# Attention with a sign layer on one core: query projections stand behind the weighing of even duos instead of between the scores of odd duos

## The chip, the core and the metric

The kernel runs on one core of one Trainium2 chip. The metric is the device time in microseconds (us) of one execution. The engines are TensorE (PE, with its weight loads as PEld), VectorE (DVE), ScalarE (ACT), GpSimd (POOL) and SyncE (SP, which issues all DMAs here).

## What is computed

Sixteen batches of 1024 rows of 256 numbers go through a layer norm, then through an attention of 16 heads of 16 columns, whose keys and values are the same for every batch, and through a dense layer whose weights are only signs. The reference, cut to what matters:

```python
xn = layernorm(x)                                  # x: (16, 1024, 256)
q = relu(xn @ Wq.T + bq); k = relu(keys @ Wk.T + bk); v = relu(values @ Wv.T + bv)
a = softmax(q_h k_h^T / 4) v_h                     # 16 heads h of 16 columns, 1024 keys
y = clip((xn @ sign(Wf).T) * scale + bias, -100, 100)
out = x + (a, laid out head by column by row, + xn) + y
```

## The kernel before, in words

**Half steps.** A batch is worked on in two half steps (`hh` 0 and 1), eight heads in each. What runs side by side in a half step belongs to different heads: the scores, exponentials and weighing of the heads `att`; the maxima of the heads after them, which the softmax of the next half step needs; the end of the heads `last`; and six or four small jobs on the next rows. Each engine has its own in-order program with a `half_step`, run for all batches from a loop (`run`, L364). With the lead-in there are 15 half steps with `hh` 0 that have scores and jobs, and 15 with `hh` 1.

**Duos.** A half step is 32 duos. The order of TensorE's work in a duo is written out in `half_step` (L766): first scores (`scores`, L588, two matmuls of 51 rows that run at once on the two halves of the array), maxima "between", second scores, maxima "before", the weighing (`weigh`, L602, eight instructions), and maxima "behind". Eight maxima, here n0 to n7 (`OCTET`, L267), are spread over an even and an odd duo by `STANDS` (L269) and `maxima_of` (L282): an even duo has n0 ahead of its weighing and n1, n2 behind it; an odd duo has n3 between the scores, n4, n5 ahead of the weighing and n6, n7 behind it. Each is one matmul of 48 rows and 512 columns (L633) into one of three banks of PSUM, the ring (L156). DVE reduces seven of the eight (L959; the one called "join" is L934, on n6), ACT takes the eighth, n2, which is a difference (L822). A matmul waits until the bank that it takes over was read, so n4 waits for the reduction of n1, and n5 for ACT on n2.

**Score tiles.** The scores go into two tiles of two banks each, used in turn, and ACT's exponentials read them (L806). A job also takes the next tile in turn (`plan`, L334; `tile`, L583), so a job behind the weighing of an even duo stands in the tile of that duo's first scores, and the odd duo's second scores wait until ACT has read the job's result.

**Jobs.** `JOBS` (L246) lists them and `JOB_DUOS` (L248) gives each its duo. With `hh` 0: four dense jobs (L677 and L679, eight matmuls of 256 columns each) and two projections of queries (L662, L664, L666, six matmuls of 512 columns each). With `hh` 1: two turns (transposes, L654) and two projections. In `plan` a turn or a projection stands between the two pairs of scores, a dense job behind the weighing. ACT copies a job's result out: L841 for a turn, L850 for a projection, L856 for a dense job. ACT's order in a duo is: first exponential, a job "between", second exponential, a job "behind", the difference n2 if the duo has it, and in the duos 9, 17, 25 and 1 a copy of the weighed sums (L813). The weighing of an even duo needs all exponentials up to the odd duo before it.

**Who else is touched.** GpSimd splits the turned rows (`split_turned`, L1145, into xnT_high and xnT_low), which the projections with `hh` 1 read, and splits the projected queries (`split_queries`, L1156) after `finish` (L1212). SyncE loads the split queries for the next heads (`load_queries`, L442), but not before the scores of duo 16 (`scored`, L543 and L547). DVE takes the reciprocals of the sums (L991) at the end of duo 7 of every half step.

The order that all this hangs on:

```python
for what in ("first", "between", "second", "behind"):
    if {"between": job and job[0] != "dense", "behind": job and job[0] == "dense"}.get(what, True):
        at[what] = tile % 2
        tile += 1
```

Of the kernel before, what the change touches and what calls it, by code (L numbers as in the profile page):

```python
# [27 lines left out]
def attention_block(nc: bass.Bass, x, keys_t, values_t, wq_t, bq, wk_t, bk, wv_t, bv, wf_t, scale, bias, out):  # L28
# [35 lines left out]
    with ctx:  # L64
        def sb(name, shape, dt):
            return ctx.enter_context(nc.sbuf_tensor(name, shape, dt))
# [34 lines left out]
        dense = sb("dense", [P, 2, BANK], FP32)  # L101
# [137 lines left out]
        def ring_order(jobs, first):  # L239
# [5 lines left out]

        JOBS = [[("dense", k, None) for k in range(2 * NA)] + [("project", a, 1) for a in range(NA)],  # L246
                [("turn", a, None) for a in range(NA)] + [("project", a, 0) for a in range(NA)]]
        JOB_DUOS = [[2, 4, 6, 8, 11, 13], [1, 3, 7, 9]]  # L248
        LEAD = 32
        ROWS_DUO = 26  # L250
        RECIP_UNIT = 14
# [30 lines left out]
        def maxima_of(d):  # L282

            n = LEAD + d // 2 * 8 + d % 2 * sum(STANDS[0])
            ends = [n + k for k in itertools.accumulate(STANDS[d % 2], initial=0)]
            return [range(*ends[k:k + 2]) for k in range(3)]
# [43 lines left out]
        def duo_job(hh, some, d):  # L330

            return JOBS[hh][JOB_DUOS[hh].index(d)] if some and d in JOB_DUOS[hh] else None

        def plan(hh, some, rows_duo):  # L334

            duos, tile, bank = [], hh * (UNITS + len(JOBS[0])), 0
            for d in range(DUOS):
                at = {}
                job = duo_job(hh, some, d)
                for what in ("first", "between", "second", "behind"):  # L340
                    if {"between": job and job[0] != "dense", "behind": job and job[0] == "dense"}.get(what, True):
                        at[what] = tile % 2
                        tile += 1
                for n in itertools.chain(*maxima_of(d)):
                    at[n] = bank % RING
                    bank += 1
                if d == rows_duo:
                    at["rows"] = bank % RING
                    bank += 1
                duos.append(at)  # L350
            assert bank % RING == 0
            return duos
# [208 lines left out]
        def _(pe):  # L561
# [204 lines left out]
            def half_step(b, hh, now, att, last, prep, ahead):  # L766
                if hh == 0:
                    next_batch()
                some = ahead or (now and hh == 0)
                for d, at in enumerate(plan(hh, some, ROWS_DUO)):  # L770
                    job = duo_job(hh, some, d)
                    between, before, behind = maxima_of(d)
                    if att:
                        scores(b, hh, att, 2 * d, at["first"])
                    if now:
                        for n in between:
                            maxima(b, hh, n, at)
                    if "between" in at:
                        do_job(b, hh, *job, at["between"])
                    if att:  # L780
                        scores(b, hh, att, 2 * d + 1, at["second"])
                    if now:
                        for n in before:
                            maxima(b, hh, n, at)
                    if last if d < 2 else att:
                        weigh(*(last if d < 2 else att), (d // 2 - 1) % QUADS, d % 2)
                    if "behind" in at:
                        do_job(b, hh, *job, at["behind"])
                    if now:
                        for n in behind:  # L790
                            maxima(b, hh, n, at)
                        if d == ROWS_DUO:
                            turn_maxima(b, hh, at["rows"])
# [5 lines left out]
        def _(act):  # L799
# [104 lines left out]
            def half_step(b, hh, now, att, last, prep, ahead):  # L904
                some = ahead or (now and hh == 0)
                for d, at in enumerate(plan(hh, some, ROWS_DUO)):
                    job = duo_job(hh, some, d)
                    if att:
                        exponentials(*att, 2 * d, at["first"])
                    if "between" in at:  # L910
                        take_job(b, hh, *job, at["between"])
                    if att:
                        exponentials(*att, 2 * d + 1, at["second"])
                    if "behind" in at:
                        take_job(b, hh, *job, at["behind"])
                    for n in itertools.chain(*maxima_of(d)):
                        if now and is_difference(n):
                            take_difference(b, hh, n, at)
                    if last and d == 1:
                        take(*last, 3)  # L920
                    if att and d % 8 == 1 and d > 1:
                        take(*att, d // 8 - 1)
                    if now and d == ROWS_DUO:
                        take_rows(b, hh, ahead, at["rows"])
# [5 lines left out]
        def _(dve):  # L930
# [142 lines left out]
            def half_step(b, hh, now, att, last, prep, ahead):  # L1073
                for d, at in enumerate(plan(hh, False, ROWS_DUO)):
                    if prep and d == AGGREGATE_DUO:
                        dve.wait_ge(s_stats, (b + 2) * 8)
                    if now:
                        for n in itertools.chain(*maxima_of(d)):
                            if prep and d in STATS_DUOS and n % 8 in STATS_AHEAD:
                                statistics(b, *ROW_TILES[2 * STATS_DUOS.index(d) + STATS_AHEAD.index(n % 8)])  # L1080
                            reduce_bank(b, hh, n, at)
                            if n >= TILES and not is_difference(n) and reductions(n - TILES) <= 5:
                                split_maxima(b, hh, reductions(n - TILES) - 1,
                                             b * 2 * REDS + made(hh, TILES - 1))
                    if last and d == RECIP_UNIT // 2:
                        reciprocals(*last)
                    if prep and AGGREGATE_DUO <= d < AGGREGATE_DUO + 4:
                        for a, j in ROW_TILES[2 * (d - AGGREGATE_DUO):2 * (d - AGGREGATE_DUO) + 2]:
                            aggregate(a, j)
# [211 lines left out]
```

## Time and profile before

| | us |
|---|---|
| median of 3 runs | 2849.71 |
| the runs | 2847.73 to 2850.22 |
| the profiled execution, its own time | 2850.59 |
| its span in the profile | 2848.8 |
| mean granted TensorE clock | 0.983 of full speed |
| busy: PE, ACT, DVE, POOL | 2770.7, 2450.2, 2337.4, 938.4 |

Busy time of PE is the union of matmuls that overlap in time and whose ends are modelled, so it tells little of how much of it could be saved. What an engine really waited for is seen better in the start times of its instructions: in the views of this document the first column is the start in us from the beginning of the span, the second the duration, and square brackets hold the idle time of that engine ahead of the instruction, and what ended it. The chain of waits is the chain of work that ended last, followed back from the end of the execution.

### The profile page before, as it was taken

The page shows a single profiled execution, that of the slowest core. Times are in us where ns is not written, and L with a number is a line of the kernel's source. Part 1 is how long each engine was busy: PE and PEld are TensorE (multiplying, and loading weights), DVE is VectorE, ACT ScalarE, POOL GpSimd, SP SyncE. Part 2 cuts the span into 40 slices and gives each one's busy share as a digit, 9 for nine tenths or more (in the row PEclk, how much of TensorE's full clock was granted, in tenths as well). Part 3 has the DMA queues.
Part 4 walks back from the last instruction along what each step waited for, and adds up shares of the span by engine and source line. Part 5 has one row for each costly group of instructions (what it writes and reads, how often), then busy time and mean ns, then how long its engine had stood idle before and what let it go on. Part 6 is the DMA issues. An engine that isn't in the chain of part 4 may idle for free.

```text
span 2848.8 us, 61155 instructions
## 1 busy us (share of the span) xinstructions
PE 2770.7 (97%) x17860; PEld 1149.8 (40%) x17860; DVE 2337.4 (82%) x4578; ACT 2450.2 (86%) x2949; POOL 938.4 (33%) x845
## 2 busy tenths in 40 slices
PE   8899999999999999999999999999999999999996
PEld 4434444443444434444443444434444443444331
DVE  6788888888888888888888888888888888888940
ACT  4688888888888888888888888888888888888996
POOL 4304334242343314333242343314333242343001
PEclk8699999999999999999999999999999999999998
DMA  7111121121221121121121221121121121211111
GB/s 142 60 40 55 65 70 36 56 70 55 65 70 52 40 70 55 65 66 33 62 69 55 65 66 49 47 70 55 65 64 35 62 68 56 65 62 37 48 55 38
DMA packets 78637, 167.74 MB, mean 59 GB/s; under 512 B 28548, under 2 KB 32647, under 8 KB 76327
## 3 DMA queue, kind: packets, MB, share of 16 engines
q1 hardware_dynamic: 78374, 164.19, 19.2%
q8 instruction: 172, 2.82, 0.4%
q14 instruction: 91, 0.74, 0.1%
HBM read 36.71 MB, written 17.83 MB: 19 GB/s over the span
## 4 chain that ended last, share of the span: by engine, by line
PE 79%; issue 10%; DVE 7%; ACT 2%; POOL 1%; DVEq 0%; DMA 0%; POOLq 0%; ACTq 0%
PE value_ps L611 30%; PE ring L633 28%; PE score_ps L597 13%; DVE mx L959 5%; ACT probs L806 2%; PE score_ps L677 1%; PE score_ps L662 1%; PE score_ps L679 1%; PE score_ps L666 1%; PE score_ps L664 1%; PE ring L720 1%; POOL fin L1097 1%; PE score_ps L715 0%; DVE excess L934 0%; PE ring L700 0%
## 5 line engine op out<-in xcount | busy, mean ns | idle before, releaser
L806 ACT ACTIVATE probs<-score_ps 128x1024 f32<-128x1024 f32 x2048 | 1992.3, 1024 | 236.1 <-PE score_ps L597 229.9
L959 DVE TENSOR_REDUCE mx<-ring 128x1 f32<-128x512 f32 x2952 | 1900.1, 684 | 248.8 <-PE ring L633 224.5
L633 PE MATMUL ring<-kstack,qstack 48*128 48x512 f32 x3444 | 1168.4, 467 | 16.7 <-DVE mx L959 3.1
L611 PE MATMUL value_ps<-probs,vones 128*32 128x512 f32 x8192 | 1092.3, 605 | 1.1 <-ACT taken L813 0.4
L633 PEld LDWEIGHTS ring<-kstack,qstack 48*128 48x128 f32 x3444 | 490.1, 184 | 1071.0 <-DVE mx L959 1034.3
L597 PE MATMUL score_ps<-qstack,kstack 51*128 51x512 f32 x4096 | 814.1, 416 | 13.8 <-ACT probs L806 4.5
L934 DVE CUSTOM_DVE_ANT_0 excess<-ring,excess 128x512 f32<-128x512 f32 x512 | 353.1, 690 | 136.7 <-PE ring L633 119.1
L1097 POOL TENSOR_TENSOR dense<-dense,affine 128x512 f32<-128x512 f32 x128 | 164.4, 1284 | 866.7 <-ACT dense L856 865.2
L597 PEld LDWEIGHTS score_ps<-qstack,kstack 51*128 51x128 f32 x4096 | 393.6, 186 | 132.1 <-ACT probs L806 70.5
L822 ACT ACTIVATE excess<-ring 128x512 f32<-128x512 f32 x492 | 294.0, 597 | 1.4 <-PE ring L633 1.2
L611 PEld LDWEIGHTS value_ps<-probs,vones 128*32 128x32 f32 x8192 | 161.5, 108 | 320.7 <-issue 289.1
L633 PE MATMUL ring<-kdiff,qstack 48*128 48x512 f32 x492 | 244.7, 497 | 0.0
L1097 POOL TENSOR_TENSOR fin<-fin 128x1024 f32<-128x1024 f32 x32 | 76.3, 2385 | 406.2 <-DMA fin<-recip 406.1
L1097 POOL TENSOR_TENSOR varp<-meanvar,const 128x8 f32<-128x8 f32 x16 | 3.2, 203 | 467.5 <-DVE meanvar L987 467.5
L1097 POOL TENSOR_TENSOR fin<-base_cur,fin 128x1024 f32<-128x1024 f32 x32 | 93.3, 2915 | 3.7 <-POOL fin L1097 2.3
L633 PEld LDWEIGHTS ring<-kdiff,qstack 48*128 48x128 f32 x492 | 90.2, 183 | 0.1
L1097 POOL TENSOR_TENSOR xnT_high<-proj,const 128x1024 fp32r<-128x1024 f32 x30 | 56.9, 1898 | 100.8 <-ACT proj L841 100.8
L991 DVE RECIPROCAL sums<-sums 128x64 f32<-128x64 f32 x32 | 17.4, 543 | 86.3 <-DMA sums<-fin 86.3
L1097 POOL TENSOR_TENSOR xin<-xin,xn 128x1024 f32<-128x1024 f32 x32 | 76.3, 2385 | 28.2 <-DVE affine L1057 28.2
L1097 POOL TENSOR_TENSOR base_new<-xin,dense 128x512 f32<-128x512 f32 x64 | 82.2, 1284 | 2.6
L813 ACT ACTIVATE taken<-value_ps 128x512 f32<-128x512 f32 x128 | 77.0, 602 | 4.9 <-PE value_ps L611 2.1
L1097 POOL TENSOR_TENSOR parts<-proj,parts 128x512 fp32r<-128x512 f32 x62 | 79.5, 1283 | 4.9
(93 smaller groups left out, 1417.2 us busy)
## 6 DMA issues: line engine op xcount, KB each, us to landing
qstack<-parts SPq DMA_DIRECT2D x768, 64.0 KB, 2.5
fin<-taken SPq DMA_DIRECT2D x256, 128.0 KB, 2.9
xin<-x SPq DMA_DIRECT2D x16, 1024.0 KB, 5.1
base_cur<-base_new SPq DMA_DIRECT2D x16, 1024.0 KB, 5.3
fin<-recip SPq DMA_DIRECT2D x32, 512.0 KB
out<-fin SPq DMA_DIRECT2D x32, 512.0 KB, 2.6
qstack<-proj SPq DMA_DIRECT2D x256, 12.0 KB
kstack<-base_cur SPq DMA_DIRECT2D x16, 128.0 KB, 6.0
```

Of the source, the lines that this page charges most:

```text
L597: mm = pe.matmul(ps[:, side * BANK:(side + 1) * BANK], kstack[rows, ah * PAIRS + pair, tc * P:(tc + 1) * P], qstack[ah][rows, pair, a * BA ...
L611: mm = pe.matmul(value_ps[h4 * 32:(h4 + 1) * 32, :], vones[:, 2 * tp + c, hh * HALF + side * PAIRS + 2 * g + j, :, :], probs[:, q % 2 * GR ...
L633: pe.matmul(ps[:, :], qstack[nh][rows, pair, st * P:(st + 1) * P], keys, start=True, stop=True).then_inc(s_mm, 1)
L662: pe.matmul(ps[:, 0:BANK], wq_high[:, ic, cols], xnT_high[:, k, ic, :], start=(ic == 0), stop=False)
L664: pe.matmul(ps[:, 0:BANK], wq_high[:, ic, cols], xnT_low[:, k, ic, :], start=False, stop=False)
L666: mm = pe.matmul(ps[:, 0:BANK], wq_low[:, ic, cols], xnT_high[:, k, ic, :], start=False, stop=(ic == IC - 1))
L806: nc.scalar.activation(probs[:, q % 2 * GROUP + u % GROUP, :], score_ps[src][:, :], ACT.Exp, scale=EXP_SCALE).then_inc(s_probs, 1)
L813: nc.scalar.activation(taken[:, a % 2, :], value_ps[:, :], ACT.Copy).then_inc(s_taken, 1)
L822: nc.scalar.activation(excess[:, :], ring[at[n]][:, :], ACT.Relu).then_inc(s_relu, 1)
L934: nc.vector.tensor_tensor_reduce(out=over, in0=second, in1=over, op0=ALU.add, op1=ALU.max, scale=1.0, scalar=LOWEST, accum_out=most).then_ ...
L959: nc.vector.tensor_reduce(most, src[:, :], AX.X, ALU.max).then_inc(s_mx, 1)
L1097: return nc.gpsimd.tensor_tensor(dst, in0, in1, op)
```

## The change

The two projections of `hh` 0 move from the duos 11 and 13 to the duos 10 and 12, those of `hh` 1 from 7 and 9 to 6 and 8. In all four cases the place in the duo changes too: from between the two pairs of scores to behind the weighing, ahead of the maxima n1 and n2. The turns and the dense jobs stay. All engines that read `plan` follow: TensorE and ACT. No instruction is added or taken away.

```diff
-        JOB_DUOS = [[2, 4, 6, 8, 11, 13], [1, 3, 7, 9]]
+        JOB_DUOS = [[2, 4, 6, 8, 10, 12], [1, 3, 6, 8]]
...
                 for what in ("first", "between", "second", "behind"):
-                    if {"between": job and job[0] != "dense", "behind": job and job[0] == "dense"}.get(what, True):
+                    if {"between": job and job[0] == "turn", "behind": job and job[0] != "turn"}.get(what, True):
                         at[what] = tile % 2
                         tile += 1
```

## Rows read from the trace of the kernel before

**Rows 1.** Head of the page: busy us and share, and the granted clock.

```profile
PE 2770.7 (97%) x17860; PEld 1149.8 (40%) x17860; DVE 2337.4 (82%) x4578; ACT 2450.2 (86%) x2949; POOL 938.4 (33%) x845
...
PEclk8699999999999999999999999999999999999998
```

**Rows 2.** Chain of waits (start, us, what), hh 0: weighings of duos 8, 10, 12, 14.

```profile
1079.82 1.00 PE value_ps L611 x8
...
1085.87 1.00 PE value_ps L611 x8
...
1092.19 1.00 PE value_ps L611 x8
...
1098.49 1.00 PE value_ps L611 x8
```

**Rows 3.** Chain of waits, hh 1: weighings of duos 4, 6, 10 and 12.

```profile
983.84 1.00 PE value_ps L611 x8
...
988.75 1.00 PE value_ps L611 x8
...
1001.77 1.00 PE value_ps L611 x8
...
1006.70 1.00 PE value_ps L611 x8
```

**Rows 4.** Timeline, duos 8 and 9 of hh 0: a dense job behind the weighing.

```profile
1079.75 1.07 PE L611 MATMUL value_ps<-probs,vones 128*32 128x512 f32 x8
...
1080.75 0.39 PE L677 MATMUL score_ps<-wf_sb,xnT_high 128*128 128x256 f32 x1
...
1081.68 0.28 PE L679 MATMUL score_ps<-wf_sb,xnT_low 128*128 128x256 f32 x1
1081.89 0.18 PEld L633 LDWEIGHTS ring<-kstack,qstack 48*128 48x128 f32 x1
...
1082.00 0.60 ACT L856 ACTIVATE dense<-score_ps 128x512 f32<-128x512 f32 x1 [0.67 <-PE score_ps L679]
...
1082.42 2.56 DVE L959 TENSOR_REDUCE mx<-ring 128x1 f32<-128x512 f32 x4 [0.82 <-PE ring L633]
...
1082.49 0.59 ACT L822 ACTIVATE excess<-ring 128x512 f32<-128x512 f32 x1
1082.65 0.19 PEld L597 LDWEIGHTS score_ps<-qstack,kstack 51*128 51x128 f32 x2 [0.23 <-ACT dense L856]
...
1082.97 1.95 ACT L806 ACTIVATE probs<-score_ps 128x1024 f32<-128x1024 f32 x2
1083.17 0.26 PEld L633 LDWEIGHTS ring<-kstack,qstack 48*128 48x128 f32 x2 [0.34 <-DVE mx L959]
```

**Rows 5.** Timeline, duo 11 of hh 0: a projection between the scores.

```profile
1087.38 0.43 PE L633 MATMUL ring<-kstack,qstack 48*128 48x512 f32 x1
...
1087.74 0.50 PE L662 MATMUL score_ps<-xnT_high,wq_high 128*128 128x512 f32 x1
...
1089.00 0.40 PE L666 MATMUL score_ps<-xnT_high,wq_low 128*128 128x512 f32 x1
1089.32 0.19 PEld L597 LDWEIGHTS score_ps<-qstack,kstack 51*128 51x128 f32 x2 [0.36 <-issue]
...
1089.49 0.69 ACT L850 ACTIVATE proj<-score_ps,bq_sb 128x512 f32<-128x512 f32 x1 [0.61 <-PE score_ps L666]
```

**Rows 6.** Timeline, duos 8 and 9 of hh 1: the reciprocals, then the wait ahead of n3.

```profile
995.00 0.16 PEld L611 LDWEIGHTS value_ps<-probs,vones 128*32 128x32 f32 x8 [0.37 <-issue]
...
995.76 0.54 DVE L991 RECIPROCAL sums<-sums 128x64 f32<-128x64 f32 x1
...
996.91 0.18 PEld L633 LDWEIGHTS ring<-kstack,qstack 48*128 48x128 f32 x1 [0.61 <-DVE mx L959]
```

**Rows 7.** Timeline of GpSimd, hh 1: the second split of turned rows.

```profile
984.69 2.38 POOL L1097 TENSOR_TENSOR xnT_low<-proj,xnT_high 128x1024 fp32r<-128x1024 f32 x1
```

**Rows 8.** Timeline of GpSimd, hh 0: the end of `finish`, ahead of the split of queries.

```profile
1091.97 2.94 POOL L1097 TENSOR_TENSOR fin<-base_cur,fin 128x1024 f32<-128x1024 f32 x1 [0.17 <-POOL fin L1097]
```

## The prediction

> **What bounds the kernel now.** I read the head of the page first: PE is busy for 97% of the span, at full clock nearly throughout [rows 1]. ACT and DVE are busy for over 80% as well, so a busy share decides nothing. Then the chain of waits, by the starts of the weighings of even duos. The distance of two of them is the length of a pair of duos, and it repeats in all 15 half steps of a kind. A plain pair takes 4.92 us: 988.75 - 983.84 = 4.91, and 1006.70 - 1001.77 = 4.93 [rows 3]. A pair with a dense job takes 1085.87 - 1079.82 = 6.05 us, the two with a projection take 6.32 and 6.30 us [rows 2]. With hh 1 the two pairs with a projection take 1001.77 - 988.75 = 13.02 us together [rows 3]; the second begins at 995.07 (995.00 in the timeline, where this weighing stands 0.07 earlier), so they take 6.32 and 6.70 us [rows 3, 6]. So a job lengthens its pair by 1.1 to 1.8 us whatever else runs, and the question is how a projection's pair looks in the new place.
>
> Third, the timeline of a dense job behind the weighing, which is the place that the projections get [rows 4]. The reader is to see that TensorE goes from weighing to job 1.00 us after the weighing's start (1079.75 to 1080.75), from job to n1 at 1081.89, and that then a fixed train runs: DVE, which the job left idle for 0.82 us, starts on n1 at 1082.42; n4 needs n1's bank and starts at 1083.17, 1.28 us after n1, having waited 0.34 us for DVE. This wait is the price of the place: the work behind the job catches up with a reduction that starts late.
>
> **The change, part by part.** Nothing is added or removed: six matmuls on TensorE and one copy on ACT move, in four duos of a batch.
>
> *TensorE.* A projection takes 1087.74 to 1089.32 = 1.58 us from its first matmul to the next work [rows 5]; the dense job takes 1080.75 to 1081.89 = 1.14 us [rows 4]. From n1 to the next pair everything in the dense pair hangs on n1 and has the same instructions. So a pair with a projection behind takes 6.05 + 1.58 - 1.14 = 6.49 us, if ACT adds nothing.
>
> *ACT.* After a projection's last matmul starts, the copy starts 0.49 us later and takes 0.69 us, and the next work of TensorE starts after 0.32 us, so the copy ends 0.49 + 0.69 - 0.32 = 0.86 us after n1 starts [rows 5]. The dense copy ends at 1082.60, 0.71 us after n1 [rows 4]. So the odd duo's second scores, held 0.23 us by the dense copy, are held 0.15 us longer. They stand ahead of n4, which had 0.34 us to wait for DVE, and this covers it. The difference n2 is queued behind the copy on ACT and comes 0.15 us later too: with the dense job it ends at 1083.08, now at n1 + 1.34 us, and n5 needs its bank, just behind n4 at n1 + 1.28. That can cost 0 to 0.06 us; I take 0.03, so 6.52 us for the pair. If that cover were gone, the full 0.15 would be paid: 6.64 us and, with a little loss at the next exponentials, 6.67 at most. The exponentials behind the difference end at about 0.6 us later than the dense pair's 1084.92, still ahead of the even weighing that needs them (1085.80 in that timeline, also 0.47 later now) [rows 2, 4].
>
> *The reciprocals.* With hh 1 DVE's 0.54 us of reciprocals fall just ahead of n1 of duo 8, DVE is late, n3 waits 0.61 us, and the projection and second scores behind n3 are late with it: this is the 6.70 against 6.32 [rows 6]. Behind the weighing the projection stands ahead of n1, TensorE is busy with it while DVE catches up, as in the dense pair of duo 8 with hh 0, whose 6.05 us contain the same reciprocals. So this 0.38 us goes away, whatever else happens.
>
> *GpSimd and SP.* The projections of hh 1 read xnT_low, written at 987.07 [rows 7]; the new place begins at about 988.68 + 1.00 = 989.7, so no wait. The split of queries comes after `finish`, which ends at 1094.9 [rows 8], past the first projection in either place, and the loads wait for the scores of duo 16. The projection issues no DMA. Moving it half a duo earlier changes nothing on either queue: cost 0, covered by some 2.5 us and by the rest of the half step.
>
> *The sum.* hh 0: 2 x 6.52 - (6.32 + 6.30) = +0.42 us. hh 1: 2 x 6.52 - 13.02 = +0.02 us. Together +0.44 a batch, 15 times: +6.6 us. The profiled execution took 2850.59 us, so 2857.2; it stands 0.9 above the median of 2849.71, on which the forecast is given: 2856.3 us. A measurement can tell about 0.2%, 5.7 us, from no change; the sum passes this where a pair takes more than 6.505 us. My floor of 6.49 gives +4.8, 6.55 gives +8.4. So the likeliest case straddles this bound.
>
> The bounds of a pair: below, the 0.34 us wait of n4 vanishes altogether, 6.49 - 0.34 = 6.15 us; above, 6.67 us.
>
> **The rivals.**
>
> *No change worth measuring.* TensorE's wait for n1's reduction shrinks by some 0.04 to 0.1 us, since in the rows it is partly the way in which waits are seen rather than work, or the copy of a projection hides. A pair takes 6.41 to 6.50: 15 x (4 x 6.41 - 25.64) = 0 to +5.4 us, 2849.7 to 2855.1. For it: the floor lies only 0.08 above break-even. Against it: from n1 to the next weighing the dense pair takes 6.05 - 2.14 = 3.91 us [rows 2, 4], and the plain one, if its n1 follows the weighing after the same 1.00 us, 4.92 - 1.00 = 3.92.
>
> *Faster: fewer changes of the array's shape.* In the old place TensorE goes from n3, a matmul on half of the rows, to the whole array and back. The step from n3 to the projection takes 0.36 us (1087.38 to 1087.74), where one within the projection takes 0.25 (five from 1087.74 to 1089.00) [rows 5]. In the new place the projection follows the weighing, which uses all rows, and TensorE enters the dense job 1.00 us after the weighing's start, as it enters maxima. So 0.11 us of TensorE's time is saved per projection. If it reached the end of each pair, and the reciprocals' 0.38 as well, a batch would gain 4 x 0.11 + 0.38 = 0.82 us: -12.3 us, 2837.4. It decides where a pair gets below 6.41 - 0.09 = 6.32 us (a gain over 5.7 us). Against it: n4 waits for DVE in the new place, so what TensorE saves ahead of it is only saved if the reduction of n1 comes earlier, and that stands behind the whole job. In the old place n1's reduction had run during the projection.
>
> The Trainium skill, page "TensorEngine Tiling (Array Packing)", Key Properties, says that changing the tiling mode, not just the tile, drains TensorE. The old place has one such change more than the new, so the rule speaks for this rival; the longer step from n3 agrees with it, but the rows cannot show that the gain reaches the pair's end.
>
> *Slower, through ACT.* The copy, the difference and two exponentials in a row push n5 and the second scores late by the full 0.15 us: 6.67 us a pair, 15 x (26.68 - 25.64) = +15.6 us, 2865.3. For it: ACT has the longest work here. Against it: the dense pair has the same queue and shows 0.34 us of room.
>
> **How the numbers follow.** Dense-like pair 6.49 to 6.55 us: 0.55, of which 0.10 lies below the 0.2% bound. No change: 0.27. Faster: 0.10. Slower through ACT: 0.08. So faster 0.10, same 0.37, slower 0.45 + 0.08 = 0.53. The range leaves out the faster case and the upper half of the ACT case: from 2848.5, a shade below no change, to 2862.5. The likeliest case alone is 2854.5 to 2858.1.
>
> **What would show it.** After the change, the weighings of duos 6, 8 and 10 with hh 1 are 6.52 us apart, and those of 10, 12, 14 with hh 0 too; the wait ahead of n4 is 0.3 to 0.4 us on DVE in these pairs; the 0.61 us wait ahead of n3 is gone; the projection's copy ends 0.86 us after n1's start; plain and dense pairs keep 4.92 and 6.05. If the pair is 6.3 or less, the train behind n1 was not fixed, and I am wrong on the sign. If plain pairs change too, something outside of my sum has moved.

## The result, and the profile after

The changed kernel takes 2855.01 us (median of 20 runs, 2852.42 to 2858.05), the kernel before 2848.93 us over 20 runs: a ratio of 1.0022, 95% interval 1.0016 to 1.0028, or 6.1 us more. The forecast was 2856.3 us from a median of 2849.7, +6.6 us, slower. The span of the profiled execution is 2853.3 us against 2848.8.

The head of the page after the change shows why it isn't the view to read: nearly the same busy times [rows 1].

```profile
PE 2781.1 (97%) x17860; PEld 1161.0 (41%) x17860; DVE 2336.9 (82%) x4578; ACT 2441.8 (86%) x2949; POOL 938.4 (33%) x845
```

The chain of waits of the changed kernel (start, us, what), weighings of the duos 6, 8, 10 of hh 1, then of the duos 8, 10, 12, 14 of hh 0:

```profile
990.92 0.99 PE value_ps L611 x8
...
997.43 0.99 PE value_ps L611 x8
...
1003.92 0.99 PE value_ps L611 x8
...
1081.82 1.00 PE value_ps L611 x8
...
1087.87 1.00 PE value_ps L611 x8
...
1094.40 1.00 PE value_ps L611 x8
...
1100.93 0.99 PE value_ps L611 x8
```

With hh 0 the two pairs with a projection take 6.53 and 6.53 us, where they took 6.32 and 6.30 [rows 2]; the dense pair keeps 6.05. With hh 1 they take 6.51 and 6.49 us, 13.00 together, where it was 13.02 [rows 3]. So hh 0 loses 0.44 us a batch, hh 1 nothing, and 15 x 0.44 is 6.6 us.

The timeline of the changed kernel, duos 10 and 11 of hh 0 (start, us, engine, line, operation; in brackets the idle time ahead and what ended it):

```profile
1087.80 1.07 PE L611 MATMUL value_ps<-probs,vones 128*32 128x512 f32 x8
...
1088.80 0.50 PE L662 MATMUL score_ps<-xnT_high,wq_high 128*128 128x512 f32 x1
...
1090.38 0.18 PEld L633 LDWEIGHTS ring<-kstack,qstack 48*128 48x128 f32 x1 [0.36 <-issue]
...
1090.55 0.69 ACT L850 ACTIVATE proj<-score_ps,bq_sb 128x512 f32<-128x512 f32 x1 [1.16 <-PE score_ps L666]
...
1090.91 2.56 DVE L959 TENSOR_REDUCE mx<-ring 128x1 f32<-128x512 f32 x4 [1.66 <-PE ring L633]
...
1091.29 0.19 PEld L597 LDWEIGHTS score_ps<-qstack,kstack 51*128 51x128 f32 x2 [0.38 <-ACT proj L850]
...
1091.66 0.30 PEld L633 LDWEIGHTS ring<-kstack,qstack 48*128 48x128 f32 x2 [0.18 <-DVE mx L959]
...
1092.20 0.16 PEld L611 LDWEIGHTS value_ps<-probs,vones 128*32 128x32 f32 x8 [0.25 <-issue]
...
998.14 0.54 DVE L991 RECIPROCAL sums<-sums 128x64 f32<-128x64 f32 x1
...
1000.28 0.19 PEld L633 LDWEIGHTS ring<-kstack,qstack 48*128 48x128 f32 x1
```

The job takes 1.58 us (1088.80 to 1090.38). DVE is idle for 1.66 us and starts on n1 0.53 us after n1's matmul; n4 starts 1.28 us after n1 as in the dense pair [rows 4]; the copy ends at 1091.24, n1 + 0.86; the second scores start at n1 + 0.91. The last two rows are the duos 8 and 9 of hh 1: the reciprocals run while the projection does, and n3 stands at 1000.28 with no wait ahead of it, where it had 0.61 us [rows 6]. With hh 1 the copy comes a little sooner: it starts at 1000.05, 0.11 us after n1 at 999.94, and ends 0.80 us after it, where with hh 0 it starts 0.17 us after n1. So the pairs with hh 1 stay at 6.49 to 6.51 us.

### The profile page after: what moved, and what is told of

Its sections match the earlier page's. It is cut to its first block, busy times and chain, and to the rows that moved or that the text cites. A ratio compares the mean times of both kernels' runs of the same rounds, so it can differ in the third digit from the quotient of the medians.

```text
span 2853.3 us, 61155 instructions
## 1 busy us (share of the span) xinstructions
PE 2781.1 (97%) x17860; PEld 1161.0 (41%) x17860; DVE 2336.9 (82%) x4578; ACT 2441.8 (86%) x2949; POOL 938.4 (33%) x845
## 4 chain that ended last, share of the span: by engine, by line
PE 81%; issue 10%; DVE 5%; ACT 2%; POOL 1%; DVEq 0%; DMA 0%; POOLq 0%; ACTq 0%
PE value_ps L611 30%; PE ring L633 29%; PE score_ps L597 14%; DVE mx L959 4%; ACT probs L806 2%; PE score_ps L677 1%; PE score_ps L662 1%; PE score_ps L679 1%; PE score_ps L664 1%; PE score_ps L666 1%; PE ring L720 1%; POOL fin L1097 1%; PE score_ps L715 0%; DVE excess L934 0%; PE ring L700 0%
## 5 line engine op out<-in xcount | busy, mean ns | idle before, releaser
L850 ACT ACTIVATE proj<-score_ps,bq_sb 128x512 f32<-128x512 f32 x64 | 44.0, 688 | 70.7 <-PE score_ps L666 69.4
```

What stands on the lines that cost most here:

```text
L850: nc.scalar.activation(proj[:, k, :], score_ps[src][:, 0:BANK], ACT.Relu, bias=bq_sb[:, oc:oc + 1]).then_inc(s_qr, 1)
```

## The experiments

In kernels with `BEHIND` in the code the line numbers are two higher: L613 is the weighing, L961 the reduction, L599 the scores, L635 the maxima, L852 the projection's copy, L808 the exponentials, L815 the copy of the weighed sums and L993 the reciprocals. The edit of `plan` that is shown first stands in all of them, but for dense_between and best_mixed.

**One half step at a time.**

```diff
-        JOB_DUOS = [[2, 4, 6, 8, 11, 13], [1, 3, 7, 9]]
+        JOB_DUOS = [[2, 4, 6, 8, 10, 12], [1, 3, 7, 9]]      # h0_behind
+        BEHIND = [(0, 10), (0, 12)]
+        JOB_DUOS = [[2, 4, 6, 8, 11, 13], [1, 3, 6, 8]]      # h1_behind
+        BEHIND = [(1, 6), (1, 8)]
...
+                    late = job and (job[0] == "dense" or (hh, d) in BEHIND)
+                    if {"between": job and not late, "behind": late}.get(what, True):
```

> Only the two projections of hh 0 are moved, to duos 10 and 12 behind the weighing; those of hh 1 stay between the scores of duos 7 and 9. If the price is the late reduction of n1 behind the job, the two pairs of hh 0 take 6.52 us each instead of 6.32 and 6.30, those of hh 1 keep 6.32 and 6.70: 15 x 0.42 = +6.3 us against the kernel before. If the loss comes from hh 1 or from the starts of the half steps, this kernel is at +0 to +2 us.

> Only the two projections of hh 1 are moved, to duos 6 and 8 behind the weighing. By the same reason the pairs take 6.51 and 6.49 us instead of 6.32 and 6.70, since the reciprocals hide under the projection: 15 x (-0.02) = -0.3 us, and some 0.1 us more a batch if the last pair of the half step stays shorter, as the trace of the changed kernel shows: -0.3 to -2 us. The rival, that each move costs the same 0.2 us whatever stands there, gives +6 us.

Only hh 0: 2854.71 us against 2849.26, ratio 1.0020 (1.0011 to 1.0029), the whole loss. Only hh 1: 2849.41 us, ratio 1.0000 (0.9991 to 1.0010). In the chain of waits of h1_behind the weighings of the duos 6, 8, 10 of hh 1 start at 988.45, 994.96 and 1001.45: 6.51 and 6.49 us, as in the changed kernel. The parts add up, +5.45 and +0.15 us against +6.1 for both, within the intervals.

**The other two places.** Between the scores of even duos (`JOB_DUOS` of the change, `plan` of before), and behind the weighing of the old odd duos:

```diff
-        JOB_DUOS = [[2, 4, 6, 8, 11, 13], [1, 3, 7, 9]]
+        JOB_DUOS = [[2, 4, 6, 8, 10, 12], [1, 3, 6, 8]]      # even_between
+        BEHIND = []
+        BEHIND = [(0, 11), (0, 13), (1, 7), (1, 9)]          # odd_behind, old JOB_DUOS
```

> All four projections in the even duos 10, 12 and 6, 8, but between the two pairs of scores. If the place behind the weighing is what costs (DVE has nothing to do during the job), here DVE has n6 and n7 to reduce during the job, and the reciprocals too: the pairs take 6.2 to 6.35 us, all four alike, and the kernel is at 15 x (4 x 6.3 - 25.64) = -6.6 us (-2 to -12). If the even duo itself costs, the pairs take 6.5 us and the kernel stands at +5 us. If changes of the array's shape counted, this place would have one more than behind the weighing and be slower than it.

> The projections in their old odd duos, but behind the weighing, ahead of n6 and n7. DVE still has n4 and n5 to reduce during the job. No maximum ahead of the next weighing waits for a bank that is read late, but the next duo's second scores come 0.58 us after n6 and must wait for ACT's copy, which ends 0.86 us after it: about +0.33 us on PE against an unstalled pair of 4.56 + 1.58. So 6.45 us (6.35 to 6.6) a pair. If what costs is only the catching up behind n1, the pairs take 6.2 us, and the kernel gains 8 us; if the place behind a weighing costs 0.2 us wherever it is, 6.5.

Both expectations failed, on the same side. even_between: 2865.71 us, ratio 1.0059 (1.0046 to 1.0073). odd_behind: 2879.20 us, ratio 1.0105 (1.0090 to 1.0121). The chain of waits of even_between, weighings of the duos 10 and 12 of hh 0:

```profile
1092.96 0.99 PE value_ps L613 x8
...
1099.67 0.99 PE value_ps L613 x8
```

A pair with a projection alone has become 1099.67 - 1092.96 = 6.71 us (the job of duo 12 stands ahead of its weighing now). The timeline of even_between, duo 10 and the n4 of duo 11:

```profile
1090.31 0.39 PE L599 MATMUL score_ps<-qstack,kstack 51*128 51x512 f32 x2
...
1090.63 0.50 PE L664 MATMUL score_ps<-xnT_high,wq_high 128*128 128x512 f32 x1
...
1092.22 0.19 PEld L599 LDWEIGHTS score_ps<-qstack,kstack 51*128 51x128 f32 x2 [0.37 <-issue]
...
1092.57 0.40 PE L635 MATMUL ring<-kstack,qstack 48*128 48x512 f32 x1
...
1095.17 0.26 PEld L635 LDWEIGHTS ring<-kstack,qstack 48*128 48x128 f32 x2 [0.52 <-DVE mx L961]
```

The plain pair of duos 10 and 11 of hh 1 in the kernel before, n1 and n4:

```profile
1002.70 0.18 PEld L633 LDWEIGHTS ring<-kstack,qstack 48*128 48x128 f32 x1 [0.84 <-DVE mx L959]
...
1003.98 0.27 PEld L633 LDWEIGHTS ring<-kstack,qstack 48*128 48x128 f32 x2 [0.45 <-DVE mx L959]
```

The job takes 1092.22 - 1090.63 = 1.59 us, and n4 behind it still waits 0.52 us for DVE, about as in a plain pair, which waits 0.45 us and has its n4 1.28 us behind n1 too. DVE had work during the job, but that wasn't the work on which TensorE waits later. The pair pays 6.71 - 4.92 = 1.79 us, the job and 0.2 more. All of it lies between the first scores and n0: 1092.57 - 1090.31 = 2.26 us, where duo 12 of the kernel before takes 1091.79 - 1091.32 = 0.47.

The chain of waits of odd_behind, weighings of the duos 10 and 12 of hh 0, and its timeline behind the job:

```profile
1097.03 0.99 PE value_ps L613 x8
...
1103.97 0.99 PE value_ps L613 x8
```

```profile
1102.33 0.19 PEld L635 LDWEIGHTS ring<-kstack,qstack 48*128 48x128 f32 x2 [0.36 <-issue]
...
1103.23 0.19 PEld L599 LDWEIGHTS score_ps<-qstack,kstack 51*128 51x128 f32 x2 [0.61 <-ACT proj L852]
```

6.94 us. The waits on n1's reduction stand ahead of the job, so none is filled, and behind it the second scores wait 0.61 us for the copy: they start 0.90 us after n6 (1102.33 to 1103.23), again the job's tile and the copy. I had expected this wait, but set it against a pair with no waits (4.56 us), though the pair's own waits lie ahead of the job and are paid before it. With hh 1 the two pairs take 6.87 and 6.88 us (weighings at 999.18, 1006.05 and 1012.93).

So a projection costs, over a plain pair of 4.92 us: between the scores of an odd duo 1.39 us, behind the weighing of an even one 1.61, between the scores of an even one 1.79, behind the weighing of an odd one 2.02, all with hh 0. It runs for 1.58.

**What holds the pair in the new place.** Three kernels from the changed one. Half of the projection's columns are not copied out (short_copy), half of the columns of n1 are not reduced in the four duos with a projection (short_n1), or both (short_both).

```diff
-                    nc.scalar.activation(proj[:, k, :], score_ps[src][:, 0:BANK], ACT.Relu,
+                    taken_cols = BANK if isinstance(b, int) and b < 0 else BANK // 2
+                    nc.scalar.activation(proj[:, k, 0:taken_cols], score_ps[src][:, 0:taken_cols], ACT.Relu,
...
-                    nc.vector.tensor_reduce(most, src[:, :], AX.X, ALU.max).then_inc(s_mx, 1)
+                    short = n % 8 == 1 and n >= LEAD and 2 * ((n - LEAD) // 8) in JOB_DUOS[hh][4 - 2 * hh:]
+                    nc.vector.tensor_reduce(most, src[:, 0:BANK // 2 if short else BANK], AX.X, ALU.max).then_inc(s_mx, 1)
```

> The changed kernel, but ACT copies only half of each projection's columns out (the other half of the projected queries is left out), which takes about 0.38 instead of 0.69 us. If n4's wait for n1's reduction sets the pair and ACT adds 0.03 us at most, the pair falls from 6.52 to 6.49 us, 1 to 2 us in all, and n4's wait for DVE grows from 0.18 to about 0.34 us. If ACT is what holds the pair, it falls by up to 0.3 us: 60 x 0.3 = -18 us.

> The changed kernel, but DVE reduces only half of the columns of n1 in the four duos with a projection (the other half of that maximum is left out): about 0.42 instead of 0.69 us. If n1's reduction alone held the train, a pair would fall by 0.27 us, 16 us in all. By the rows ACT's copy is just behind it: second scores at n1 + 0.91, n4 0.34 later, n5 at n1 + 1.39 after the difference. So the pair falls by no more than 0.03 to 0.05 us, 2 to 3 us in all, and the wait ahead of n4 is then small or ended by ACT.

> Both of the two together (half of the projected columns and half of each such n1 left out). If two chains of nearly equal length, n1's reduction and ACT's copy with the difference behind it, hold the train, only this one gains: n4 at about n1 + 1.0, the pair 6.24 us (6.2 to 6.35), 60 x -0.28 = -17 us against the changed kernel, 2838 us. If the train is held by TensorE's own work or by the changes of the array's shape, it gains no more than 3 us here too.

The inserted lines move some line numbers: the reduction is L960 in short_copy, the copy L851 in short_copy and short_both. Measured beside the kernel before at 2849.61 us: 2853.45, 2853.45 and 2845.66 us; ratios 1.0015 (1.0006 to 1.0024), the same, and 0.9986 (0.9977 to 0.9995). So they stand at +3.8, +3.8 and -4.0 us, where the changed kernel stood at +6.1 in its own series. Either alone gains some 2 us, too little to be told apart here, and both together some 10. The timelines, duos 10 and 11 of hh 0, of short_copy:

```profile
1087.82 0.18 PEld L633 LDWEIGHTS ring<-kstack,qstack 48*128 48x128 f32 x1 [0.36 <-issue]
...
1089.10 0.26 PEld L633 LDWEIGHTS ring<-kstack,qstack 48*128 48x128 f32 x2 [0.40 <-DVE mx L960]
```

of short_n1:

```profile
1090.18 0.18 PEld L633 LDWEIGHTS ring<-kstack,qstack 48*128 48x128 f32 x1 [0.36 <-issue]
...
1091.09 0.19 PEld L597 LDWEIGHTS score_ps<-qstack,kstack 51*128 51x128 f32 x2 [0.38 <-ACT proj L850]
...
1091.58 0.18 PEld L633 LDWEIGHTS ring<-kstack,qstack 48*128 48x128 f32 x1 [0.19 <-ACT excess L822]
```

and of short_both:

```profile
1088.41 0.18 PEld L633 LDWEIGHTS ring<-kstack,qstack 48*128 48x128 f32 x1 [0.36 <-issue]
...
1088.58 0.48 ACT L851 ACTIVATE proj<-score_ps,bq_sb 128x256 f32<-128x256 f32 x1 [1.16 <-PE score_ps L666]
...
1088.98 0.60 ACT L822 ACTIVATE excess<-ring 128x512 f32<-128x512 f32 x1
...
1089.42 0.39 PEld L633 LDWEIGHTS ring<-kstack,qstack 48*128 48x128 f32 x2
...
1090.05 0.16 PEld L611 LDWEIGHTS value_ps<-probs,vones 128*32 128x32 f32 x8 [0.24 <-issue]
```

With a short copy n4 stands at n1 + 1.28 us as before, and now waits 0.40 us for DVE: the copy wasn't what held n4. With a short reduction the wait on DVE is gone, but the second scores still wait for the copy, and the last wait is that of n5 for ACT's difference, at n1 + 1.40: the pair keeps all but 0.02 us. With both, n4 starts at n1 + 1.01 and the next weighing at n1 + 1.64, where it was 1.82 (1090.38 to 1092.20): 0.18 us a pair. I had put 0.28: a half copy takes 0.48 us and not 0.38, and the difference behind it ends at 1089.58, so n5 is then the last. The next weighing starts 0.47 to 0.48 us after the end of ACT's difference in the changed kernel, in short_n1 and in short_both, and 0.50 us after n4 in short_copy (1089.10 to 1089.60) and in the dense pair of the kernel before. So two chains start at the job's end, over DVE and over ACT, and are equal in length to within some hundredths of a microsecond; with hh 0 ACT's is the longer one.

**The dense jobs in the old place of the projections.**

```diff
-        JOB_DUOS = [[2, 4, 6, 8, 11, 13], [1, 3, 7, 9]]
+        JOB_DUOS = [[1, 3, 5, 7, 11, 13], [1, 3, 7, 9]]
+        BEHIND = []
...
+                    late = job and ((hh, d) in BEHIND)       # a dense job too is "between" now
```

> The kernel before, but the four dense jobs too stand between the scores of odd duos (1, 3, 5, 7 instead of 2, 4, 6, 8 behind the weighing). If the place between n1 and n4 is cheap because a job there fills the wait for n1's reduction, which a plain pair has as well, a dense pair takes 4.92 + 1.14 + 0.2 - 0.4 = 5.85 us instead of 6.05: 4 x 15 x -0.2 = -12 us (-8 to -15). If the old place suited only the projections, or every job costs its own length plus 0.2 us, it takes 6.05 us or more, and the kernel gains nothing.

2845.09 us, ratio 0.9986 (0.9977 to 0.9995): a gain of some 4 us, not 12. The chain of waits, weighings of the duos 4, 6 and 10 of hh 0:

```profile
1065.73 0.99 PE value_ps L613 x8
...
1071.66 0.99 PE value_ps L613 x8
...
1082.73 0.99 PE value_ps L613 x8
```

A dense pair takes 5.93 us, 0.12 less than behind the weighing; the timeline has the second scores of duo 3 wait for ACT:

```profile
1062.86 0.18 PEld L599 LDWEIGHTS score_ps<-qstack,kstack 51*128 51x128 f32 x2 [0.20 <-ACT probs L808]
```

The dense job is short, so ACT's exponential of the first scores, whose tile the second scores take, isn't done when TensorE comes back. And from duo 6 to duo 10 it takes 1082.73 - 1071.66 = 11.07 us, of which a dense pair has 5.93: the pair of duos 8 and 9, plain now, takes 5.14 us instead of 4.92. DVE's reciprocals had been hidden by the dense job in duo 8. Four times 0.12 less 0.22 is 0.26 us a batch, 4 us in all.

**The reciprocals.** They are moved to the end of duo 9 in the kernel before (`RECIP_UNIT` 18 for 14).

> The kernel before, with DVE's reciprocals at the end of duo 9 instead of duo 7. If they are what lengthens the second pair with a projection of hh 1, that pair (duos 8, 9) falls from 6.72 to 6.32 us and the plain pair behind it (duos 10, 11) rises from 4.92 to about 5.15; with hh 0 the pair of duos 10, 11, a projection between the scores, rises from 6.32 to about 6.7. In all 15 x (-0.40 + 0.23 + 0.40) = +3.5 us. If the copy of the weighed sums in duo 9 is the cause instead, the pair of duos 8, 9 stays at 6.7 us.

2852.33 us against 2849.47, ratio 1.0014 (1.0005 to 1.0023). The timeline, weighings of the duos 8, 10 and 12 of hh 1, and the reciprocals:

```profile
994.28 0.16 PEld L613 LDWEIGHTS value_ps<-probs,vones 128*32 128x32 f32 x8 [0.35 <-issue]
...
1000.60 0.16 PEld L613 LDWEIGHTS value_ps<-probs,vones 128*32 128x32 f32 x8 [0.37 <-ACT taken L815]
...
1001.37 0.54 DVE L993 RECIPROCAL sums<-sums 128x64 f32<-128x64 f32 x1
...
1005.74 0.16 PEld L613 LDWEIGHTS value_ps<-probs,vones 128*32 128x32 f32 x8 [0.37 <-issue]
```

The pair with the projection in duo 9 takes 6.32 us and not 6.70 [rows 3, 6], the plain one behind it 5.14. The whole is 2.9 us slower, near the +3.5 expected. The third part of that sum is there too. The chain of waits of recip_9, weighings of the duos 10 and 12 of hh 0:

```profile
1082.80 1.00 PE value_ps L613 x8
...
1089.52 0.99 PE value_ps L613 x8
```

6.72 us, where it was 6.32 [rows 2]. The copy of the weighed sums in duo 9 stayed where it was, and the pair with it takes what a pair without one takes.

**Putting the pieces together.** One projection moved (mixed_8), then the best place for every job (best_mixed).

```diff
-        JOB_DUOS = [[2, 4, 6, 8, 11, 13], [1, 3, 7, 9]]
+        JOB_DUOS = [[2, 4, 6, 8, 11, 13], [1, 3, 7, 8]]      # mixed_8
+        BEHIND = [(1, 8)]                                    # dense jobs behind as before
+        JOB_DUOS = [[1, 3, 5, 8, 11, 13], [1, 3, 7, 8]]      # best_mixed
+        BEHIND = [(0, 8), (1, 8)]                            # and no other job behind, as in dense_between
```

> The kernel before with one projection moved: the second of hh 1 from duo 9, between the scores, to duo 8 behind the weighing. The pair falls from 6.72 to 6.49 us: 15 x -0.23 = -3.4 us. By the rival that the place behind the weighing costs 0.2 us whatever runs on DVE, it costs +3 us.

> Jobs between the scores of odd duos, except in duo 8, where the reciprocals want cover: dense jobs in 1, 3, 5 between and 8 behind the weighing, projections of hh 0 in 11 and 13 as before, those of hh 1 in 7 between and 8 behind. By the measured pairs: hh 0 gains 3 x (6.05 - 5.93) = 0.36 us, hh 1 gains 6.72 - 6.49 = 0.23 us, 15 x 0.59 = -9 us against the kernel before (-6 to -11). If pairs were not additive, it stays within 4 us of the kernel with the dense jobs in odd duos.

mixed_8: 2846.96 us against 2849.47, ratio 0.9991 (0.9982 to 1.0000), 2.5 us less where 3.4 were expected, at the edge of what is told apart. best_mixed: 2841.11 us, ratio 0.9974 (0.9964 to 0.9983): 8 us faster than the kernel before, where 9 were expected, and some 14 faster than the changed one. Its chain of waits, weighings of the duos 4, 6, 8 and 10 of hh 0: 5.92 us with a dense job between the scores, 4.90 plain, 6.05 with the dense job behind duo 8's weighing, which hides the reciprocals.

```profile
1068.75 0.99 PE value_ps L613 x8
...
1074.67 0.99 PE value_ps L613 x8
...
1079.57 0.99 PE value_ps L613 x8
...
1085.62 1.00 PE value_ps L613 x8
```

## Why the prediction was right, point by point

- *The price from the dense pair.* 6.05 + 1.58 - 1.14 = 6.49 us, and 0.03 for ACT: 6.52. Measured 6.53 and 6.53 us with hh 0, 6.51 and 6.49 with hh 1. The job behind the weighing keeps everything after it at n1 plus a fixed time. The 0.03 for ACT is needed with hh 0 alone; with hh 1, where the copy comes sooner, the pairs stand near the floor of 6.49.
- *ACT.* The copy at n1 + 0.86 us and the second scores 0.15 us later hit to 0.01 us. The short kernels show that this chain is as long as DVE's. What failed is a sign that I named: the wait ahead of n4 shows 0.18 us and not 0.3 to 0.4. The scores ahead of it came 0.15 us later, so 0.34 - 0.15 = 0.19 us was left of the wait, which my own working says, while n4 stood where it had stood. And these 0.34 us weren't the room that ACT had. In the dense pair the difference ends at 1083.08 and the weighing starts at 1083.67, where ACT's chain alone would allow 1083.08 + 0.48 = 1083.56: a room of 0.11 us. The projection's 0.15 goes over it by 0.04.
- *The reciprocals.* Their 0.38 us with hh 1 went away, and made up for what the two moves cost there. recip_9 moved the delay by moving them.
- *The sum.* +6.6 us by the pairs, +6.1 (4.6 to 8.0) measured. The profiled span grew by 4.5 only, so that the total came within 0.5 us of the sum is in part luck. The last pair of the half steps with hh 1 got shorter. The chain of waits of the kernel before, weighings of the duo 30 and the next duo 0:

```profile
1051.33 1.00 PE value_ps L611 x8
...
1056.74 0.99 PE value_ps L611 x8
```

and of the changed kernel:

```profile
1053.48 1.00 PE value_ps L611 x8
...
1058.74 1.00 PE value_ps L611 x8
```

  5.41 and 5.26 us. This happens far from the projections, where the loop goes round; no instruction there changed. TensorE waits for the exponentials ahead of the first scores of duo 0, 0.55 us in the kernel before and 0.39 in the changed one. I had nothing for it in the sum. From one batch to the next this pair varies by some 0.1 us in every kernel; its median is 5.41 us in the kernel before and 5.32 in the changed one, some 1.5 us in all. It is 5.34 in h0_behind and 5.41 in h1_behind, where I had expected the gain; it stays at 5.41 in odd_behind, recip_9 and mixed_8 as well, and is 5.33 to 5.36 in the other kernels, all of which have a job with hh 0 in another duo. So it goes with the jobs of hh 0; why stays open.
- *The rival of the array's shape.* The Trainium skill, page "TensorEngine Tiling (Array Packing)", Key Properties, has a change of the tiling mode drain TensorE. The rows agree with a price: in even_between a job between row-halved matmuls costs 0.2 us beyond its 1.59, and the step into it takes 0.32 us. So the rival's 0.11 us a projection was too small rather than too large, and the saving did reach the pair's end: 6.71 us between the scores of an even duo, 6.53 behind its weighing. But the rival's time, a gain of 12 us, did not come, since the move also gave up the wait that the old place filled. By the costs of the four places that is 1.79 - 1.39 = 0.40 us, of the 0.45 that TensorE waits ahead of n4 in a plain pair.
- *No change.* The slowdown is clear of zero, but the interval of 0.16 to 0.28% doesn't settle whether it passes the 0.2% that I had set. The rival's mechanism, a shrinking wait of TensorE for n1's reduction, isn't there: n4 stands at n1 + 1.28 us in the changed kernel as in the dense pair. The pairs with hh 1 do lie in the rival's band or at its edge, but because ACT adds next to nothing there.

What I had not understood is why the old place was cheap. I called the wait ahead of n4 the price of the place behind the weighing. A plain pair has that wait too, and a job behind the weighing of an even duo costs little but its length: 1.57 to 1.61 us for a projection of 1.58, 1.13 for a dense job of 1.14. The old place was the special one. I wrote that n1's reduction had run during the projection there, but then expected in two experiments that any work for DVE during the job would do. It is that one reduction: a plain pair already has TensorE wait ahead of n4, and a job between n1 and n4 fills that wait. There it costs 1.39 us for 1.58 of work; in the three other places tried it costs its length or more. dense_between, where dense jobs put into that place got cheaper, bears this out; a plain pair with a shorter reduction of n1 was not run.

## What to carry to other kernels

Look for the wait that the steady pattern already has, and put extra work on the waiting engine inside it: after the producer's instruction, ahead of the consumer's. Giving the other engine something else to do meanwhile didn't help here. When a like job stands in the place that you consider, its measured pair plus the difference in length is a good forecast: here it hit to hundredths of a microsecond. Then look at the next-longest chain, since an idle time in a trace overstates the room when something else is about to arrive late too.

## What the hardware showed that was not expected

The copy of half as many columns takes 0.48 us where the whole takes 0.69, so 0.27 us of it don't depend on columns, if time grows evenly with them. A job that uses the whole array between two matmuls on halves of it cost TensorE about 0.2 us beyond its own stream (1.79 against 1.59 in even_between). TensorE seems to wait for no engine there: the idle time ahead of the job is put down to ACT's exponentials in duo 10, but it is as long in duo 12, where it is "issue". That the array's shape is the cause is likely and not shown, since no run has such a job without the change of shape. Behind the weighing, which works on all rows, the job costs its stream alone.
